# Twelve weight buffers instead of eight, expert rows requested earlier, and the last chunk's routing in five lumps instead of ten

## The reference, cut to what matters

```python
def _L1_ffn_ref(x, ln1_w, ln2_w, wq, wk, wv, wo, router_w, w1, w2, w3):
    ...
    x = x + y @ wo.T
    flat = _rmsnorm(x, ln2_w).reshape(-1, Cx)
    probs = jax.nn.softmax(flat @ router_w.T, axis=-1)
    tp, ti = jax.lax.top_k(probs, TOPK)
    tp = tp / (jnp.sum(tp, axis=-1, keepdims=True) + 1e-09)
    weights = jnp.sum(tp[..., None] * jax.nn.one_hot(ti, NE, dtype=flat.dtype), axis=1)
    out = jnp.zeros_like(flat)
    for e in range(NE):
        hh = jax.nn.silu(flat @ w1[e].T) * (flat @ w3[e].T)
        out = out + weights[:, e:e + 1] * (hh @ w2[e].T)
    return x + out.reshape(Bx, Tx, Cx)
```

## Time and profile before

| | |
|---|---|
| median of 3 runs | 582.17 us (581.45 to 585.45) |
| the profiled execution | 581.81 us |
| its span on the core | 580.1 us, 11403 instructions |
| TensorE busy in the span | 484.3 us, 83% |
| VectorE busy | 433.7 us, 75% |
| ScalarE busy | 318.3 us, 55% |
| GpSimd busy | 258.4 us, 45% |
| moved by DMA | 91.66 MB |
| chain that ended last | PE 55%, DVE 20%, DMA 11%, ACT 5%, issue 5% |

### The profile page before, as it was taken

One profiled execution on the slowest core, in us unless ns is written; L12 is line 12 of the kernel. 1 busy time (PEld: TensorE's weight loads), 2 busy tenths in 40 slices (PEclk: granted clock), 3 DMA queues, 4 the chain that ended last, 5 costly groups with the idle time before them and its releaser, 6 DMA issues.

```text
span 580.1 us, 11403 instructions
## 1 busy us (share of the span) xinstructions
PE 484.3 (83%) x3849; PEld 272.3 (47%) x3849; DVE 433.7 (75%) x1069; ACT 318.3 (55%) x532; POOL 258.4 (45%) x281
## 2 busy tenths in 40 slices
PE   1999994879999979998776768889899976778880
PEld 1533332557777745454332223233353235678880
DVE  6897965887999993575779588799987416877664
ACT  0677796876999900110114454466549636567760
POOL 3000002513544540110236389599936575677562
PEclk9999996889999999999958898999999987999996
DMA  7999964200014925011023332200031472799986
GB/s 292 394 423 421 421 245 173 92 1 20 22 36 189 409 63 110 0 42 27 14 73 98 91 111 79 75 2 1 1 113 34 155 300 69 227 281 346 376 270 222
DMA packets 39570, 91.66 MB, mean 158 GB/s; under 512 B 7488, under 2 KB 24944, under 8 KB 35168
## 3 DMA queue, kind: packets, MB, share of 16 engines
q1 hardware_dynamic: 35072, 85.20, 42.1%
q0 software_dynamic: 2272, 4.69, 2.2%
q10 hardware_dynamic: 2176, 1.13, 0.7%
HBM read 69.39 MB, written 19.23 MB: 153 GB/s over the span
## 4 chain that ended last, share of the span: by engine, by line
PE 55%; DVE 20%; DMA 11%; ACT 5%; issue 5%; SPq 2%; POOL 2%; POOLq 0%; DVEq 0%; ACTq 0%
DVE A L2358 8%; PE ps L1561 8%; PE ps L1738 7%; PE ps L1472 7%; PE ps L1489 6%; PE ps L1387 5%; DMA R<-in_adj_in 5%; PE ps L1730 3%; PE ps L1841 3%; PE ps L1639 3%; DMA R<-slots_in 2%; PE ps L1586 2%; PE ps L1857 1%; PE ps L1364 1%; DVE bst L1889 1%
## 5 line engine op out<-in xcount | busy, mean ns | idle before, releaser
L2358 DVE TENSOR_REDUCE A<-ps 128x1 f32<-128x512 f32 (+3 forms) x160 | 86.2, 602 | 12.7 <-PE ps L1639 12.1
L1285 ACT ACTIVATE A<-ps 128x1024 f32<-128x1024 f32 (+3 forms) x80 | 68.4, 892 | 40.1 <-PE ps L1730 39.9
L977 POOL TENSOR_TENSOR G<-G,A 128x1024 f32<-128x1024 f32 (+3 forms) x40 | 74.2, 1894 | 8.3 <-ACT A L1285 8.2
L1639 PE MATMUL ps<-A 96*128 96x512 f16 (+3 forms) x160 | 54.5, 378 | 10.7 <-DVE A L2358 4.7
L1387 PE MATMUL ps<-R,G 128*128 128x512 f32 x128 | 59.2, 605 | 1.9 <-ACT R L1100 1.0
L1561 PE MATMUL ps<-A,G 128*128 128x512 f32 x128 | 59.9, 594 | 0.0
L1489 PE MATMUL ps<-R 128*128 128x128 f16 x768 | 48.4, 220 | 6.8 <-DVE x L2050 5.8
L1489 PEld LDWEIGHTS ps<-R 128*128 128x128 f16 x768 | 45.4, 98 | 14.3 <-issue 6.6
L2032 DVE SCALAR_TENSOR_TENSOR R<-R 128x512 f16<-128x512 f32 x64 | 46.6, 751 | 6.9 <-ACT R L1140 6.7
L1472 PE MATMUL ps<-G,R 128*128 128x512 f16 x192 | 48.9, 391 | 1.3 <-ACT R L1140 1.2
L1138 ACT ACTIVATE R<-ps,b 128x512 f32<-128x512 f32 x64 | 44.1, 688 | 10.6 <-PE ps L1472 9.6
(11 more groups left out here) (310 smaller groups left out, 934.1 us busy)
## 6 DMA issues: line engine op xcount, KB each, us to landing
A<-w_split SPq DMA_DIRECT2D x39, 533.0 KB, 6.6
A<-in_adj_t SPq DMA_DIRECT2D x16, 1024.0 KB, 17.5
slots_in<-xn SPq DMA_DIRECT2D x1, 8320.0 KB, 22.4
R<-in_adj_in SPq DMA_DIRECT2D x7, 1024.0 KB, 5.3
xn<-in_adj_in SPq DMA_DIRECT2D x5, 1024.0 KB
w_split<-A SPq DMA_DIRECT2D x9, 533.0 KB, 3.3
xT<-in_adj_in SPq DMA_DIRECT2D x4, 1024.0 KB, 12.6
A<-in_f_w SPq DMA_DIRECT2D x16, 170.5 KB
```

The source lines that it names most:

```text
L977: pool.tensor_tensor(total, total, probabilities(n, pair)[:, :, t0:CW], ALU.add).then_inc(s_sum, 1)
L1285: act.activation(probabilities(n, pair)[:, :, t0:CW], ps[:, 2 * pair:2 * pair + 2, t0:CW], ACT.Exp, scale=1.0 / (SQ * SQ * float(HD) ** 0. ...
L1639: last = pe.matmul(ps[:, bank, 0:width], queries(t // TPC, h)[0:KQ, P * (t % TPC):P * (t % TPC) + P], keys(b, h // (NH // NKV))[0:KQ, 0:wi ...
L2358: dve.reduce_max(pm[:, h, t % TPC, b:b + 1], ps[:, bank, 0:width], AX_X).then_inc(s_rmf, 1)
```

## The change

It sets the number of weight buffers to 12. The four new ones are tiles 15, 14, 4 and 5 of `A`, and the row buffers in tiles 4 and 5 move to those tiles' ends to make room. Weights 0 to 7 are asked for where they were. Weights 8 to 11 no longer wait for an output product, but for the end of attention and for the last reads of tiles 14 and 15 (`s_pv`, `s_squares`, `s_rmf`), and stand in front of the rows of slots 9 to 12 and 13 to 16, two each. From then on the rows of a batch are asked for ahead of the weights two batches back. The late slots' table is read as soon as the weights of slot 16 are issued. The pair loads at the end go into weight buffers 3 to 6.

The late tiles' 43 routing steps are cut at 13, 23, 33 and 38 into five lumps behind k = 2 to 6. TensorE's ranks move from k = 4 to k = 3, the router's exponential on ScalarE from k = 3 to k = 2. `low_hidden` of slots 3 and 4 moves from GpSimd to VectorE. On GpSimd the first two output scatters move behind the late row scatters.

```diff
--- before.py
+++ after.py
@@ -246,8 +246,8 @@
         v2 = A[:, 8:10, CW:CW + 3 * D].rearrange("p s (k d) -> p s k d", k=3)
         split1 = A16[:, 12:14, 0:WSPLIT]
 
-        WB = 8
-        w1s = [A16[:, 6 + n, 0:WSPLIT] for n in range(WB)]
+        WB, EARLY_WB = 12, 8
+        w1s = [A16[:, j, 0:WSPLIT] for j in (*range(6, 14), 15, 14, 4, 5)]
         first_part = lambda part: slice(2 * H1 * part, 2 * H1 * part + 2 * H1)
         second_part = lambda part: slice(W13 + 3 * D * part, W13 + 3 * D * part + 3 * D)
 
@@ -259,9 +259,9 @@
             return (second_rows if which else first_rows)[:, t, :]
 
         G_flat = G[:, :, :].rearrange("p t d -> p (t d)")
-        HOMES = [(15, G_flat), (6, A[:, 4, 2 * CW:]), (4, A[:, 5, 2 * CW:]), (14, R[:, ROWS_AT:])]
+        HOMES = [(15, G_flat), (6, A[:, 4, T - 6 * RW:]), (4, A[:, 5, T - 4 * RW:]), (14, R[:, ROWS_AT:])]
         homes = [home[:, RW * n:RW * n + RW] for count, home in HOMES for n in range(count)]
-        assert len(homes) == SLOTS and ROWS_AT + HOMES[-1][0] * RW <= 4 * T
+        assert WSPLIT // 2 <= T - 6 * RW and len(homes) == SLOTS and ROWS_AT + HOMES[-1][0] * RW <= 4 * T
         XB = 6
         BATCHES = (1, 2, 3, 3, 4, 4, 1, 3, 4, 4, 4, 4, 2)
         ENDS = [sum(BATCHES[:b + 1]) for b in range(len(BATCHES))]
@@ -294,7 +294,9 @@
             return A[:, n // 16, P * (n % 16):P * (n % 16) + P]
 
         def pair_rows(c):
-            return A[:, 14 + c // 2, 2 * CW * (c % 2):2 * CW * (c % 2) + 2 * CW]
+            n = OPEN_END - NC - 1 + c
+            assert SLOTS - WB <= n < OPEN_END
+            return A[:, 6 + n % WB, 0:2 * CW]
 
         def free_cols(c, a, n):
 
@@ -468,8 +470,9 @@
 
         AGAIN = 16
         CLAMPED = "an early block is full and lies in its expert's region, a late one is bounded by the table's last step"
-        weights_base = [*[AGAIN] * 6, *[16 * sum(row_buffer(i) == b for i in range(NT)) for b in range(2)]]
-        s_xr, s_w1l = [*s_A[0:4], s_A[10], s_A[15]], [*s_A[4:10], *s_row[0:2]]
+        STACKED = 16 * 3 * (NH + NKV) // 2
+        weights_base = [*[AGAIN] * 6, *[16 * sum(row_buffer(i) == b for i in range(NT)) for b in range(2)], *[STACKED] * NC]
+        s_xr, s_w1l = [*s_A[0:4], s_A[10], s_A[15]], [*s_A[4:10], *s_row[0:2], *s_stack]
         assert len(s_xr) == XB and len(s_w1l) == WB
         s_squares, SQUARES = s_first, 16 * 3
         s_empty, s_ld1, s_attw = s_A[11], s_A[12:14], s_A[14]
@@ -595,13 +598,13 @@
 
         inverse_rows = A[:, 14, 0:CW]
         PREPARE_AT = {(0, 1): 0, (0, 2): 1, (0, 3): 2, (1, 2): 3, (1, 5): 4, (2, 4): 5, (2, 8): 6, (3, 4): 7}
-        OUT_FIRST = 2
+        OUT_FIRST = 0
         ON_SCALAR = 2
-        LOW_ON_POOL = 5
-        LOW_IN_FRONT = 5
+        LOW_ON_POOL = 3
+        LOW_IN_FRONT = 3
         PACE = 2 * (len(steps) - len([c for c, _ in steps if c == NC - 1]) + 11)
         LOW_AT = {(0, 1): 0, (0, 2): 1, (1, 0): 2, (1, 2): 3, (1, 5): 4}
-        STEP_BOUNDS = (0, 6, CHOSEN, 21, POSITIONED, 32, 35, 38, 40, 42, ROUTE_STEPS[2])
+        STEP_BOUNDS = (0, CHOSEN, WEIGHED, 33, 38, ROUTE_STEPS[2])
         STEPS_AT = {2 + n: ends for n, ends in enumerate(zip(STEP_BOUNDS, STEP_BOUNDS[1:]))}
 
         block = ctx.enter_context(nc.Block())
@@ -810,22 +813,34 @@
                 read_blocks(b)
             for s in range(2):
                 sp.wait_ge(s_wst[s], AGAIN + 16 * (E1 // 2 + s))
-            for n in range(WB):
+            for n in range(EARLY_WB):
                 load_weights(n)
+            for b in range(4, batch_of[FIRST]):
+                read_blocks(b)
             sp.wait_ge(s_negT, NC)
             sp.wait_ge(s_od, NC - 1)
             for b in range(4):
                 load_slot_rows(b)
-            for n in range(WB, ENDS[3]):
+            sp.wait_ge(s_pv, len(steps))
+            sp.wait_ge(s_squares, SQUARES + 1)
+            sp.wait_ge(s_rmf, unit_no[("db", NC - 1)] + 1)
+            for b in range(4, batch_of[FIRST]):
+                for n in range(EARLY_WB + 2 * (b - 4), EARLY_WB + 2 * (b - 3)):
+                    load_weights(n)
+                load_slot_rows(b)
+            for n in range(WB, FIRST):
                 load_weights(n)
-            for b in range(4, len(BATCHES)):
+            late = batch_of[FIRST]
+            for b in range(late, len(BATCHES)):
                 read_blocks(b)
-                if ENDS[b] - BATCHES[b] == FIRST:
+                if b == late:
                     load_weights(FIRST)
                 load_slot_rows(b)
-                for n in range(ENDS[b] - BATCHES[b], ENDS[b]):
-                    if n != FIRST:
+                if b > late + 1:
+                    for n in range(ENDS[b - 2], ENDS[b - 1]):
                         load_weights(n)
+            for n in range(ENDS[-2], SLOTS):
+                load_weights(n)
             sp.wait_ge(s_scat[0], 16 * OPEN_END)
             for c in range(NC - 1):
                 load_pairs(c)
@@ -1339,7 +1354,7 @@
                     high_of_rows(NC - 1)
                 if k + 1 < SLOTS:
                     slot_high(k + 1)
-                if k == 3:
+                if k == 2:
                     router_exp(2, TILES[2])
                 if k >= 4:
                     copy_output(k - 4)
@@ -1871,7 +1886,7 @@
                     unit(("tr", NC - 1))
                 if k == 1:
                     unit(("logit", NC - 1))
-                if k == 4:
+                if k == 3:
                     unit(("rank", 2))
                 if k >= 3:
                     output1(k - 3)
```

## The result

Over 19 runs each the changed kernel takes 578.66 us (median, 576.55 to 581.70) and the kernel before 581.45 us (579.56 to 585.45). The ratio is 0.9954, with a 95% interval of 0.9939 to 0.9969; the medians are 2.8 us apart, half a per cent. The forecast was 578.5 us. The profiled execution took 577.97 us, with a span of 576.1 (before 581.81 and 580.1).

A forecast was written before the change was run, and what follows sets the result against it. It took VectorE to bound the slots up to slot 14, then full DMA (share 0.99). Slot 38 3.6 us earlier, tail unchanged: span 580.1 - 3.6 = 576.5, plus 1.7 is 578.2; with 0.36 for the median, 578.5 us, range 576.0 to 582.3.

The forecast's parts named there:

- four signs of being wrong: DMA share well under 1 (517 to 550), last scatters not waiting for ScalarE, clock 0.50 behind 508, slot 14 after 517.5.
- The front costs +1.2 us (0.8 to 1.9): Slots 3 and 4: low parts moved to VectorE add 1.7 us; less GpSimd interference gives back up to 0.9.
- Five lumps cost nothing extra: Late tiles' routing on VectorE: each lump blocks slots longer, 1.3 to 5 us, but the sum stays the same.
- Late row scatters from 499.9 to 510.1, SyncE standing till 512, weights 18 to 20 at 517: GpSimd and SyncE before slot 17: the weak place, DMA having little to do between 506 and 517.
- Four more buffers are worth only about one slot's weights.: Loads by 517: weights 0 to 17 in place, against the same 17 issued at about 516 before; some rows besides.
- DMA from 517 on: 39.3 us, ended at 556.3, slot 38 at 559.0: Weights, rows and scatters take 39.3 us; 2 us to land and 0.7 for what the count misses give 559.0.
- The bound that I put 0.7 us lower, 558.3: Slot 38's start by TensorE and VectorE alone: 562.8, less 5.7 of waits, plus 1.2 for the front.
- The page's rule: Slot loads: 2.0 us plus bytes at 436 GB/s, 1.56 us a slot, so DMA would not bound; that rival's chance 0.15.
- The tail stays 17.3 us: From slot 38's hidden product to the span's end: unchanged, GpSimd's scatters hidden with 4 us to spare.
- It needs 1.40 us each when it runs behind: GpSimd's output scatters: at 1.40 us each slot 35's could go at 559.1, wanted at 563.1.
- The rival: GpSimd's output scatters become the bound: at 1.62 us each slot 35's goes 3.7 us late, time 582.2; chance 0.12.
- The clock: Rival: TensorE's clock stays low after its 3.7 us stand, 1.6 us a slot if past 508.5, 583.1 us; chance 0.08.

The follow-up runs named there:

- short_low_2: Changed kernel with VectorE's low part of the hidden values cut from 384 to 16 columns from slot 8 on; ratio 0.9924 to the kernel before.
- half_weights_before_2: Kernel before the change, with only half of the weights' columns loaded in slots 17 to 38; ratio 0.9926 to the kernel before.
- after: The whole change against the kernel before, in the first comparison; median 578.66 us, ratio 0.9954.
- after_again: The changed kernel once more, unaltered, on chip 1, one of the longer-running chips; 614.76 us against 612.44 for the kernel before there, ratio 1.0036.

## Why the prediction was right, point by point

The mechanism of the gain was right: more is loaded before the late slots, and TensorE's stands for rows and weights go. Two terms of the sum were wrong, the landing of the last weights and the pace of GpSimd's scatters, and they were wrong in opposite ways. Of the four signs of being wrong that the prediction named, one came: the last scatters run without a wait for ScalarE. The expected waits of TensorE for DMA behind slot 30 and GpSimd's catching up by slot 29 did not come.

- **Nothing changes ahead of the slots.** Right: slot 0 at 482.15 for 482.27.
- **Table at 508.5, 5.9 us earlier.** It ended at 507.14, 7.3 us earlier. The rounds were counted rightly. VectorE's steps ran with less of GpSimd's work beside them than before (GpSimd stood 4.70 us here), which is the likely rest; it was not tried apart.
- **The front costs +1.2 us (0.8 to 1.9).** From slot 0 to slot 14's transpose it was 33.81 us for 32.97: +0.84, the cheap end. But this execution didn't have the fall of the clock at slot 9. With it the front costs 2.5 us (short_low_2), and the term's range was too narrow for that.
- **Five lumps cost nothing extra.** Right as a sum: slots 0 to 8 cost 4.8 us more, slots 8 to 17 give 4.9 back, of which about 1.0 is the wait for slot 17's rows and not the lumps'. What I did not see is what the lumps do to the loads: with eight buffers they cost DMA 1.3 MB in the first 34 us.
- **Late row scatters from 499.9 to 510.1, SyncE standing till 512, weights 18 to 20 at 517.** Measured 499.58 to 509.70, rows of slot 17 at 511.53, weights at 517.53. Right to half a microsecond. But the prediction left DMA "little to do" between 506 and 517, and its share there was 0.68. The weak place cost TensorE nothing: its one stand behind slot 16 is of 0.20 us and inside slot 19's product.
- **"Four more buffers are worth only about one slot's weights."** Roughly right in bytes (0.9 MB, a slot's set and rows are 0.6), wrong in the reason: measured against the lumps without buffers they are worth 2.2 MB. I had costed both halves as if they added up; alone neither gives anything that can be told from zero.
- **DMA from 517 on: 39.3 us, ended at 556.3, slot 38 at 559.0.** The work was sized well: the last packet of weights ended at 556.35. The 2 us to land and the 0.7 "for what the count misses" were the error: slot 38's product started at 557.50 without a wait, so that landing took no more than 1.15 us (in the kernel before the last packet ended at 561.82, 0.96 us ahead of that product). The bound that I put 0.7 us lower, 558.3, was the one that ruled, TensorE's and VectorE's own pace: less the 0.4 by which the front was cheaper, and less 1.0 of the stand of 1.16 us in slot 19, of which 0.20 was left, it gives 556.9. The 0.6 that is missing is in small delays, of 0.2 us each in slots 24 and 28 above all.
- **The page's rule.** The Trainium skill, "DMA: Bandwidth & Descriptors", section "Anatomy of one DMA — SWDGE (gpsimd) path", gives its 436 GB/s for DMAs that GpSimd issues, and the prediction used it for loads that SyncE issues. By it the transfers would not have bounded the slots at all. The kernel before says otherwise: with half of the weights slots 17 to 38 are 5.2 us shorter (half_weights_before_2). The changed kernel moves 363 GB/s at a share of 0.98, so DMA is still full there; what has changed is how much is loaded ahead.
- **The tail stays 17.3 us.** Wrong by 1.3 us, and this is the step that failed: "It needs 1.40 us each when it runs behind". Up to slot 35 it needed 1.49 (from 510.01 to 562.14), which takes 3.0 of the 4 us to spare. The other 1.7 went because slot 38 started that much earlier than foreseen, so slot 35's scatter came 0.7 us late. Another 0.8 us came from the last four, three of which start under VectorE's additions of the pairs; the prediction has no term for that. Together the last scatter is 1.6 us late. The 1.40 was taken from a stretch in which the slots had stands, and a longer round of VectorE breaks the step between its low part and GpSimd's scatter. Where the rounds are even the scatters stay in step, at 1.61. How long they do is chance in part: half_weights_before_2, also without stands, needed 1.42 (24 steps from 507.29 to 541.40), and there rounds of 1.68 and 1.77 us were enough to end the step. The rival had the mechanism and its threshold (1.51), but no mixture. Its chance, 0.12, was for the whole price.
- **The clock.** It fell behind the stand in front of the ranks and was back by 498, hidden as foreseen. The second fall, behind the last lump, was not in the forecast; where it came it cost 1.6 us in all and not for each slot. The 583.1 us of that rival don't follow from its terms: four slots and a half at 1.6 us, less the 0.7 by which the other bound was higher, are 6.5 us and give 585.0.

## What to carry to other kernels

Two halves of a change that work on the same queue should not be costed one by one: first ask which event each load waits for, and what the other half does to that event. When stands are removed from a pipeline, the engines beside it lose the gaps in which they caught up; price their work at the pace without stands, and look for two engines whose periods are then the same. And a tail that is made of the last few outputs copied together has a floor that no earlier work moves (17.2 to 18.0 us here).

## What the runs showed of the hardware

- A GpSimd indirect scatter takes 0.97 us and 0.30 behind it. It takes longer if it starts under VectorE's fp32 subtraction of 128x384 with both inputs in SBUF (0.56 us): 1.07 with 0.22 us of that left, 1.31 with 0.47 left. With that operation on 16 columns it took 0.97 in all 30 cases. When the slots' period is 1.62 us, this makes a stable step of 1.61 us, which a round of 1.85 us ended (after) and one of 1.68 too (half_weights_before_2).
- Chips differ by 4 to 5% on this program (581.2 to 582.4 us on three of the experiments' chips, 607.5 and 612.4 on two), and all of the difference lies behind the first indirect scatter. On the slower ones TensorE's signals come up to 1.49 us late (after_again). A verdict of half a per cent from one kind of chip says nothing of the other.
- The same stand of 2.4 us lowers the granted clock in some executions and not in others: 3 of 5 profiles.
